# Two-layer transformer block on one core: one exp and one maximum for a pair of heads, and PSUM banks from a plan

## The chip, the cores and the metric

The kernel runs on one core of a Trainium2 chip. The metric is the device time of one execution in microseconds. Its engines are TensorE (PE; PEld is its weight load), VectorE (DVE), ScalarE (ACT), GpSimd (POOL), and SyncE (SP), which issues most transfers. TensorE writes its results into PSUM, which has eight banks of 512 fp32 values per partition.

## The reference

The input is x, 4 x 1024 x 128 in fp32. Two layers follow each other, and both add two branches to x that read the same normalized xn:

```python
xn = _layernorm(x)
x = x + _L0_attn_ref(xn, ...) + _L0_ffn_ref(xn, ...)
xn = _layernorm(x)
x = x + _L1_attn_ref(xn, ...) + _L1_ffn_ref(xn, ...)
```

Layer 0's attention has 16 heads of 8 dimensions, rotary Q and K, scores / sqrt(8), a softmax over 1024 keys, weights times V, and an output projection with bias. Its feed-forward is a mixture of 8 experts (128 to 512 to 128, Relu), of which each token uses the best two, weighted by a softmax. Layer 1's attention has the same heads, no rotation, and is causal. Its feed-forward is gated (silu(gate) * up, 352 wide), with inputs and weights rounded to FP4 in blocks of 16 with a scale per block.

## The kernel before, in words

A class `Plan` writes out the order of all work by hand rules before anything is emitted. The work of each batch and layer is a phase; there are eight, in the order `PHASES` (layer, batch): (0,0), (0,1), (1,0), (0,2), (1,1), (0,3), (1,2), (1,3). The kernel is a list of 491 slots, and every engine goes through the slots in order.

A slot can hold a *step* and a *quad*, and 436 of them hold both; 12 slots ahead of the first step hold a quad at most, and 12 at the end no quad.

- A step (`scores`, L930) is the scores of four heads (a group g) for one tile of 128 keys and 512 queries: four matmuls of kind E, keys on the partitions, each into a bank of its own. `exps` (L790) on ScalarE turns each into weights in `PR`. The step's product with V (PV, eight matmuls into the bank `pO`, which is no part of the round) comes one slot later and waits for all four exps. In layer 1 the tiles on the diagonal are narrower (512, 384, 256, 128 columns), and two small matmuls per pair add the mask.
- A quad is the same four heads with queries on the partitions, and serves the row maxima, 12 slots ahead of the steps that need them: four matmuls of kind M (`maxima` on TensorE, L955), and four reductions (`maxima` on VectorE, L1137) into `mparts`. In layer 1 the quads on the diagonal add the mask in the same operation (L1153) and write to `junk`. The finished maxima (`combine`, `mtr`) are put under the queries in `QX` by small transfers, so that the scores come out with the maximum subtracted.
- Everything else that passes through PSUM is an item of `xs`: projections (`pj`), the values (`v`), the experts' first and second product (`unit`, `y`), gate and up (`gu`), transposes (`xT`, `mtr`, `fin`, `of`, `turn`), and so on. Over both kinds of engine that empty them, 93 of the 436 slots have none, 173 one, 152 two and 18 three. `unit` is emptied by four Relu operations on ScalarE, `y` by one copy.

TensorE's order in a slot: E of heads 0 and 1, M of heads 0 and 1, PV of the step before, E of heads 2 and 3, M of heads 2 and 3, then the slot's `xs`. ScalarE's: exps 0 and 1, what the slot has besides, exps 2 and 3, evacuations. VectorE's: maxima 0 and 1, small steps, maxima 2 and 3, `combine`, small steps, evacuations.

Seven banks (`RING = 7`, tiles `ring0` to `ring6`) serve E, M and `xs`. `number` lists all fills in TensorE's order in `plan.ring`, and the bank of an item is its place in that list modulo 7. `vacant` (L918) makes TensorE wait until the item seven places earlier has been emptied: for an exp (`s_ex`), a maximum (`s_mr`) or an evacuation (`s_freed`). For a pair both waits stand ahead of both matmuls.

Of the kernel before, what the change touches and what calls it, by code (L numbers as in the profile page):

```python
# [34 lines left out]
class Plan:  # L35
# [214 lines left out]
    def number(self):  # L250
        self.steps, self.quads, self.outs, self.mtrs, self.combines, self.masks = {}, {}, {}, {}, {}, {}
        self.xs, self.by, self.fins, self.ring = {}, {}, {}, []
        self.parts, self.parts0, self.pools = {}, {}, {}
        self.at = {"E": {}, "M": {}, "X": {}}
        taken = {"A": 0, "D": 0}
        mid = 0
        for s in self.slots:
# [11 lines left out]
            for pair in range(2):  # L269
                for kind, key, n in (("E", s["step"], self.steps), ("M", s["quad"], self.quads)):  # L270
                    if key is not None:
                        for j in (2 * pair, 2 * pair + 1):
                            k = 4 * n[key] + j
                            self.at[kind][k] = len(self.ring)
                            self.ring.append((kind, k))
            for e in s["xs"]:
# [4 lines left out]
                taken[who] += 1  # L281
                self.at["X"][k] = len(self.ring)
                self.ring.append(("X", e))
# [9 lines left out]
            for e in s["pool"]:  # L293
                if e[0] == "round" and e[-1] == POOL_STEPS - 2:
                    self.pools[e[1:-1]] = len(self.pools)

    def bank(self, kind, k):
        return self.at[kind][k] % RING

# [4 lines left out]
def two_layer_block(nc, x, wqa0, wqb0, wka0, wkb0, wv0, wo0, gate_w, gate_b, w1, b1, w2, b2wo,  # L304
# [27 lines left out]
    with ctx:  # L332
# [3 lines left out]
        def ps(name, width):  # L336
            return ctx.enter_context(nc.psum_tensor(name, [P, width], f32))
# [91 lines left out]

        ring = [ps(f"ring{i}", HALF) for i in range(RING)]  # L430
        pO = ps("pO", HALF)
# [86 lines left out]
        def wide(t, n):  # L518
            return t[:, 0:n // BLK].rearrange("p (n o) -> p n o", o=1).to_broadcast([P, n // BLK, BLK])

        def bank(e):
            return ring[plan.bank("X", plan.xs[e])]

# [25 lines left out]
        with nc.Block() as block:  # L549
# [235 lines left out]
            def _(act):  # L785
# [4 lines left out]
                def exps(s, js):  # L790
# [12 lines left out]
                    if n >= 2:  # L803
                        act.wait_ge(s_pv, n - 1)
                    for j in js:
                        k = 4 * n + j
                        act.wait_ge(s_e, k + 1)
                        nc.scalar.activation(PR[:, n % 2, HALF * j + off:HALF * j + HALF],  # L808
                                             ring[plan.bank("E", k)][:, off:HALF], ACT.Exp,
                                             scale=SCALE).then_inc(s_ex, 1)  # L810

# [103 lines left out]
            def _(pe):  # L915
                pe.wait_ge(s_wA, 16 * len(loads_a))

                def vacant(kind, k):  # L918

                    r = plan.at[kind][k] - RING  # L920
                    if r >= 0:
                        was, of = plan.ring[r]
                        if was == "E":
# [46 lines left out]
                for s in plan.slots:  # L970
# [24 lines left out]
                    for e in s["xs"]:  # L995
                        vacant("X", plan.xs[e])
                        dst = bank(e)
# [120 lines left out]
            def _(dve):  # L1118
# [18 lines left out]
                def maxima(s, js):  # L1137
                    if s["quad"] is None:
                        return
                    p, g, qt, kh = s["quad"]  # L1140
                    layer = PHASES[p][0]
                    for j in js:
                        k = 4 * plan.quads[s["quad"]] + j
# [3 lines left out]
                        dve.wait_ge(s_m, k + 1)  # L1147
                        if layer == 0 or P * (qt + 1) > HALF * (kh + 1):
                            v.tensor_reduce(dst, src[:, 0:w], axis=X, op=ALU.max).then_inc(s_mr, 1)  # L1149
                        else:  # L1150
                            if k >= 2:
                                dve.wait_ge(s_mr, k - 1)
                            v.tensor_tensor_reduce(out=junk[k % 2][:, 0:w], in0=src[:, 0:w],  # L1153
                                                   in1=diag[:, HALF - w:HALF], scale=1.0, scalar=NEG,
                                                   op0=ALU.add, op1=ALU.max, accum_out=dst).then_inc(s_mr, 1)

# [350 lines left out]
```

## Time and profile before

| | |
|---|---|
| time, median of 3 runs | 1646.52 us (1646.3 to 1650.8) |
| the profiled execution's own time, and its span | 1650.6 us, 1648.9 us |
| PE busy | 1477.5 us (90%) |
| PEld busy | 623.0 us (38%) |
| DVE busy | 1342.0 us (81%), 3450 instructions |
| ACT busy | 1131.9 us (69%), 2612 instructions |
| POOL busy | 579.7 us (35%) |
| mean granted TensorE clock | 0.944 of full speed |

Busy times are the union of an engine's instructions, as shares of the span. A PE that is busy isn't PE at its peak, since the ends of its matmuls are modelled. In the listing by line a helper's line (L504, L507, L510) stands for all that call it; the tiles tell them apart: `ring<-QX,KX 50*128` is an E matmul, `ring<-KX,QX 48*128` an M matmul, `pO<-PR,VX` is PV, L808 the exps, L1149 and L1153 the maxima.

### The profile page before, as it was taken

To read this page: it belongs to the slowest core of one execution; us is meant where nothing else is said; L and a number is where in the kernel's file an instruction comes from. 1 tells how busy PE (TensorE), PEld (TensorE's weight loads), DVE (VectorE), ACT (ScalarE), POOL (GpSimd) and SP (SyncE) were. 2 spreads that over 40 slices of the span, in tenths; PEclk is the share of its full clock that TensorE was granted. 3 is DMA by queue.
4 is the path that set the end of the run, shared out by engine and by line. 5 is a ranking of instruction groups with operands and counts; after the bars stand their busy time and mean duration, and the time that the engine had idled before them with its cause. 6 is when DMAs were issued, how large, how long until landed. Compare 5 with 4: busy or idle time off the path is not lost.

```text
span 1648.9 us, 34553 instructions
## 1 busy us (share of the span) xinstructions
PE 1477.5 (90%) x10685; PEld 623.0 (38%) x10685; DVE 1342.0 (81%) x3450; ACT 1131.9 (69%) x2612; POOL 579.7 (35%) x532
## 2 busy tenths in 40 slices
PE   3688989997999999998999999989999989889996
PEld 1121334442434554433343444334444433334432
DVE  7999877786887778898888878879887878887990
ACT  2167678786788556777878756767887845766675
POOL 4003302003063353733434361221624473644520
PEclk8599999998999989999999999999999987999998
DMA  8202264323263135231711225223462100500000
GB/s 246 56 7 60 78 164 116 89 80 89 55 180 96 35 113 127 69 89 49 185 39 44 63 61 152 66 82 103 147 137 65 39 24 1 154 2 15 2 2 14
DMA packets 162915, 131.80 MB, mean 80 GB/s; under 512 B 30825, under 2 KB 130098, under 8 KB 162738
## 3 DMA queue, kind: packets, MB, share of 16 engines
q1 hardware_dynamic: 158642, 121.19, 27.2%
q0 software_dynamic: 4096, 8.40, 1.7%
q8 instruction: 93, 1.52, 0.4%
q14 instruction: 84, 0.69, 0.1%
HBM read 88.50 MB, written 40.50 MB: 78 GB/s over the span
## 4 chain that ended last, share of the span: by engine, by line
PE 64%; DVE 18%; ACT 6%; issue 5%; POOL 4%; DMA 1%; SPq 1%; another core or an unknown queue 0%; DVEq 0%; ACTq 0%; POOLq 0%
PE ring L504 41%; PE pO L504 19%; DVE mparts L1149 10%; PE ring L507 4%; ACT PR L808 4%; DVE junk L1153 1%; ACT hid L875 1%; DVE xn L1216 1%; DVE xr L1329 1%; DVE hs L1441 1%; DVE stats L1199 1%; DVE hs L1440 1%; POOL rstd L700 1%; POOL ra L707 0%; POOL parts L715 0%
## 5 line engine op out<-in xcount | busy, mean ns | idle before, releaser
L808 ACT ACTIVATE PR<-ring 128x512 f32<-128x512 f32 (+3 forms) x1792 | 875.9, 557 | 279.8 <-PE ring L504 267.1
L1149 DVE TENSOR_REDUCE mparts<-ring 128x1 f32<-128x512 f32 x1280 | 806.8, 682 | 122.1 <-PE ring L504 108.6
L504 PE MATMUL pO<-PR,VX 128*18 128x512 f32 (+3 forms) x3584 | 444.7, 569 | 9.2 <-ACT PR L808 8.5
L504 PE MATMUL ring<-KX,QX 48*128 48x512 bf16 (+3 forms) x1792 | 339.4, 373 | 82.3 <-ACT PR L808 32.4
L504 PE MATMUL ring<-QX,KX 50*128 50x512 bf16 (+3 forms) x1792 | 335.7, 371 | 36.7 <-DVE mparts L1149 20.3
L504 PEld LDWEIGHTS ring<-QX,KX 50*128 50x128 bf16 x1792 | 89.6, 93 | 481.7 <-DVE mparts L1149 175.2
L1153 DVE CUSTOM_DVE_ANT_0 junk<-ring,diag 128x384 bf16<-128x384 f32 (+3 forms) x512 | 227.8, 486 | 53.6 <-PE ring L504 46.3
L504 PEld LDWEIGHTS ring<-KX,QX 48*128 48x128 bf16 x1792 | 96.5, 94 | 181.5 <-DVE mparts L1149 54.1
L758 POOL TENSOR_SCALAR bq<-bq 128x352 f32<-128x352 f32 (+1 forms) x40 | 47.1, 1177 | 333.9 <-ACT bq L912 322.7
L731 POOL DMA_INDIRECT rows_in<-xn,at x64 | 62.6, 978 | 257.2 <-PE pO L504 166.0
L875 ACT ACTIVATE hid<-ring,b1r 128x128 f32<-128x128 f32 x368 | 104.9, 369 | 36.8 <-PE ring L504 36.2
L747 POOL DMA_INDIRECT ra<-rows_out,at x64 | 61.0, 953 | 170.8 <-PE pO L504 125.5
L504 PEld LDWEIGHTS pO<-PR,VX 128*18 128x18 f32 x3584 | 60.7, 97 | 142.3 <-issue 108.0
L504 PE MATMUL ring<-yx,w1r 128*128 128x128 f32 x736 | 108.0, 291 | 6.9 <-DMA b1r<-in_b 6.3
L504 PEld LDWEIGHTS ring<-yx,w1r 128*128 128x128 f32 x736 | 92.6, 197 | 31.6 <-issue 19.0
L504 PE MATMUL ring<-w2r,hid 128*128 128x128 f32 x736 | 99.2, 279 | 0.0
L504 PEld LDWEIGHTS ring<-w2r,hid 128*128 128x128 f32 x736 | 95.3, 200 | 0.9 <-ACT PR L808 0.9
L510 ACT ACTIVATE yx<-ring 128x256 f32<-128x256 f32 (+1 forms) x96 | 36.2, 377 | 58.1 <-PE ring L504 48.3
L504 PE MATMUL ring<-identb,laterb 128*128 128x128 bf16 x512 | 74.8, 229 | 0.0
L767 POOL TENSOR_TENSOR bq<-hq,bq 128x352 f32<-128x352 f32 x64 | 59.8, 934 | 4.8
L772 POOL TENSOR_SCALAR yq<-yq 128x352 f32<-128x352 f32 (+1 forms) x40 | 60.3, 1506 | 3.3
L715 POOL TENSOR_TENSOR parts<-rb,parts 128x512 bf16<-128x512 f32 x30 | 34.7, 1155 | 74.0 <-ACT parts L510 74.0
(164 smaller groups left out, 1406.1 us busy)
## 6 DMA issues: line engine op xcount, KB each, us to landing
scratch<-parts SPq DMA_DIRECT2D x96, 256.0 KB, 3.7
w1r<-in_w SPq DMA_DIRECT2D x92, 256.0 KB
w2r<-in_w SPq DMA_DIRECT2D x92, 256.0 KB
QX<-scratch SPq DMA_DIRECT2D x128, 96.0 KB, 3.2
KX<-scratch SPq DMA_DIRECT2D x64, 192.0 KB, 4.0
xg<-rows_in SPq DMA_DIRECT2D x92, 64.0 KB
rows_out<-yx SPq DMA_DIRECT2D x92, 64.0 KB
QX<-mT SPq DMA_DIRECT2D x256, 2.0 KB
```

Of the source, the lines that this page charges most:

```text
L504: return nc.tensor.matmul(dst, lhsT, rhs, start=start, stop=stop, **kw)
L507: return nc.tensor.transpose(dst, src, ident[0:src.shape[0], 0:src.shape[0]])
L510: return nc.scalar.activation(dst, src, ACT.Copy)
L731: nc.gpsimd.indirect_dma_start(xs[b % 2], bass.IndirectOffsetOnAxis(at[b % 2][:, c:c + 1], 0), xn[0][:, c % T, :], None).then_inc(s_sc[b], 16)
L747: nc.gpsimd.indirect_dma_start(yg[:, D * t:D * t + D], None, ys[b % 2], bass.IndirectOffsetOnAxis(at[b % 2][:, c:c + 1], 0)).then_inc(s_yg ...
L758: ins = nc.gpsimd.tensor_scalar(b_, b_, 1.0, None, ALU.max)
L767: ins = nc.gpsimd.tensor_tensor(b_, dst, b_, ALU.subtract)
L772: ins = nc.gpsimd.tensor_scalar(y, y, SHIFT, SHIFT, ALU.add, ALU.subtract)
L808: nc.scalar.activation(PR[:, n % 2, HALF * j + off:HALF * j + HALF], ring[plan.bank("E", k)][:, off:HALF], ACT.Exp, scale=SCALE).then_inc( ...
L875: ins = nc.scalar.activation(hid[N % 2][:, P * fc:P * fc + P], src[:, P * fc:P * fc + P], ACT.Relu, bias=b1r[N % 2][:, fc:fc + 1])
L1149: v.tensor_reduce(dst, src[:, 0:w], axis=X, op=ALU.max).then_inc(s_mr, 1)
L1153: v.tensor_tensor_reduce(out=junk[k % 2][:, 0:w], in0=src[:, 0:w], in1=diag[:, HALF - w:HALF], scale=1.0, scalar=NEG, op0=ALU.add, op1=ALU ...
```

## The change: one operation for two heads, and a placed pair of banks

- The seven banks become one tile `ring` of 7 x 512 columns; `both` gives a view [128, 2, n] over the banks of items k and k+1.
- `exps` issues one activation over two banks where it issued two, waits for both score matmuls, and counts `s_ex` up by two when it ends.
- `maxima` on VectorE issues one reduction over [128, 2, 512] into two columns of `mparts`, except for layer 1's quads on the diagonal, which stay as they were. 320 of the 448 quads are not on the diagonal. `s_mr` goes up by two. The places of the maxima within `mparts` are the same as before.
- `place_banks` replaces the fixed round. A unit is a pair (two neighbouring banks) or an item of `xs` (one bank). For each unit in TensorE's order `choose` tries the four places that were given out longest ago, looks ahead over the next five units in all, and takes the place with the least sum of max(0, 4 - ago) squared, where ago is the number of units since a bank of the place was last given out. `was` keeps, for each item, what its bank held before, and `vacant` waits for that.

Orders of work, matmuls, transfers and their placement in slots are not changed.

```diff
--- before.py
+++ after.py
@@ -251,7 +251,7 @@
         self.steps, self.quads, self.outs, self.mtrs, self.combines, self.masks = {}, {}, {}, {}, {}, {}
         self.xs, self.by, self.fins, self.ring = {}, {}, {}, []
         self.parts, self.parts0, self.pools = {}, {}, {}
-        self.at = {"E": {}, "M": {}, "X": {}}
+        self.banks = {}
         taken = {"A": 0, "D": 0}
         mid = 0
         for s in self.slots:
@@ -271,7 +271,6 @@
                     if key is not None:
                         for j in (2 * pair, 2 * pair + 1):
                             k = 4 * n[key] + j
-                            self.at[kind][k] = len(self.ring)
                             self.ring.append((kind, k))
             for e in s["xs"]:
                 who = "D" if e[0] in ("pj", "lg", "rt", "mtr", "fin", "gu", "down", "fp") else "A"
@@ -279,7 +278,6 @@
                 self.xs[e] = k
                 self.by[e] = (who, taken[who])
                 taken[who] += 1
-                self.at["X"][k] = len(self.ring)
                 self.ring.append(("X", e))
                 if e[0] == "fin":
                     self.fins[e[1:]] = len(self.fins)
@@ -293,9 +291,40 @@
             for e in s["pool"]:
                 if e[0] == "round" and e[-1] == POOL_STEPS - 2:
                     self.pools[e[1:-1]] = len(self.pools)
+        self.place_banks()
 
     def bank(self, kind, k):
-        return self.at[kind][k] % RING
+        return self.banks[kind, k]
+
+    def choose(self, used, units, now):
+
+
+        if not units:
+            return 0, None
+        width = units[0]
+        places = sorted(range(RING - width + 1), key=lambda b: max(used[b:b + width]))[:4]
+        best = None
+        for b in places:
+            ago = now - max(used[b:b + width])
+            then = used[:b] + [now] * width + used[b + width:]
+            cost = max(0, 4 - ago) ** 2 + self.choose(then, units[1:], now + 1)[0]
+            if best is None or cost < best[0]:
+                best = cost, b
+        return best
+
+    def place_banks(self):
+
+        units = [self.ring[i:i + (1 if self.ring[i][0] == "X" else 2)] for i in range(len(self.ring))
+                 if self.ring[i][0] == "X" or self.ring[i][1] % 2 == 0]
+        used, holds = list(range(-RING, 0)), {}
+        self.banks, self.was = {}, {}
+        for now, unit in enumerate(units):
+            b = self.choose(used, [len(u) for u in units[now:now + 5]], now)[1]
+            for i, item in enumerate(unit):
+                self.banks[item] = b + i
+                self.was[item] = holds.get(b + i)
+                holds[b + i] = item
+                used[b + i] = now
 
 
 PLAN = Plan()
@@ -427,7 +456,8 @@
         xqT = sb("xqT", [P, S])
         hqT = sb("hqT", [P, FC1, P])
 
-        ring = [ps(f"ring{i}", HALF) for i in range(RING)]
+        ring_all = ps("ring", RING * HALF)
+        ring = [ring_all[:, HALF * i:HALF * i + HALF] for i in range(RING)]
         pO = ps("pO", HALF)
 
         s_x0 = [sem(f"s_x{i}") for i in range(B)]
@@ -518,8 +548,13 @@
         def wide(t, n):
             return t[:, 0:n // BLK].rearrange("p (n o) -> p n o", o=1).to_broadcast([P, n // BLK, BLK])
 
+        def both(kind, k, lo, hi):
+
+            a, b = plan.bank(kind, k), plan.bank(kind, k + 1)
+            return ring_all[:, :].rearrange("p (b n) -> p b n", n=HALF)[:, a:b + 1, lo:hi]
+
         def bank(e):
-            return ring[plan.bank("X", plan.xs[e])]
+            return ring[plan.bank("X", e)]
 
         def filled(e):
             return plan.xs[e] + 1
@@ -802,12 +837,11 @@
                         act.wait_ge(s_x, filled(("wT", 2)))
                     if n >= 2:
                         act.wait_ge(s_pv, n - 1)
-                    for j in js:
-                        k = 4 * n + j
-                        act.wait_ge(s_e, k + 1)
-                        nc.scalar.activation(PR[:, n % 2, HALF * j + off:HALF * j + HALF],
-                                             ring[plan.bank("E", k)][:, off:HALF], ACT.Exp,
-                                             scale=SCALE).then_inc(s_ex, 1)
+                    k = 4 * n + js[0]
+                    act.wait_ge(s_e, k + 2)
+                    dst = PR[:, n % 2, HALF * js[0]:HALF * js[0] + 2 * HALF].rearrange("p (j n) -> p j n", n=HALF)
+                    nc.scalar.activation(dst[:, :, off:HALF], both("E", k, off, HALF), ACT.Exp,
+                                         scale=SCALE).then_inc(s_ex, 2)
 
                 for s in plan.slots:
                     exps(s, (0, 1))
@@ -917,9 +951,8 @@
 
                 def vacant(kind, k):
 
-                    r = plan.at[kind][k] - RING
-                    if r >= 0:
-                        was, of = plan.ring[r]
+                    if plan.was[kind, k]:
+                        was, of = plan.was[kind, k]
                         if was == "E":
                             pe.wait_ge(s_ex, of + 1)
                         if was == "M":
@@ -993,7 +1026,7 @@
                     scores(s, 1)
                     maxima(s, 1)
                     for e in s["xs"]:
-                        vacant("X", plan.xs[e])
+                        vacant("X", e)
                         dst = bank(e)
                         if e[0] == "xT":
                             _, p, h = e
@@ -1139,20 +1172,23 @@
                         return
                     p, g, qt, kh = s["quad"]
                     layer = PHASES[p][0]
+                    if layer == 0 or P * (qt + 1) > HALF * (kh + 1):
+                        k, i = 4 * plan.quads[s["quad"]] + js[0], TH * (js[0] // 2) + qt % TH
+                        dve.wait_ge(s_m, k + 2)
+                        v.tensor_reduce(mparts[layer][:, qt // TH, i:i + 2 * TH + 1:2 * TH, kh], both("M", k, 0, HALF),
+                                        axis=X, op=ALU.max).then_inc(s_mr, 2)
+                        return
                     for j in js:
                         k = 4 * plan.quads[s["quad"]] + j
                         w = HALF if layer == 0 else min(HALF, P * (qt + 1) - HALF * kh)
                         dst = mparts[layer][:, qt // TH, TH * (2 * (j % 2) + j // 2) + qt % TH, kh:kh + 1]
                         src = ring[plan.bank("M", k)]
                         dve.wait_ge(s_m, k + 1)
-                        if layer == 0 or P * (qt + 1) > HALF * (kh + 1):
-                            v.tensor_reduce(dst, src[:, 0:w], axis=X, op=ALU.max).then_inc(s_mr, 1)
-                        else:
-                            if k >= 2:
-                                dve.wait_ge(s_mr, k - 1)
-                            v.tensor_tensor_reduce(out=junk[k % 2][:, 0:w], in0=src[:, 0:w],
-                                                   in1=diag[:, HALF - w:HALF], scale=1.0, scalar=NEG,
-                                                   op0=ALU.add, op1=ALU.max, accum_out=dst).then_inc(s_mr, 1)
+                        if k >= 2:
+                            dve.wait_ge(s_mr, k - 1)
+                        v.tensor_tensor_reduce(out=junk[k % 2][:, 0:w], in0=src[:, 0:w],
+                                               in1=diag[:, HALF - w:HALF], scale=1.0, scalar=NEG,
+                                               op0=ALU.add, op1=ALU.max, accum_out=dst).then_inc(s_mr, 1)
 
                 def weight_step(k):
 
```

## Rows read from the trace of the kernel before

**Rows 1.** The page: span, busy us (share) and instructions, shares of the chain.
```profile
span 1648.9 us, 34553 instructions
...
PE 1477.5 (90%) x10685; PEld 623.0 (38%) x10685; DVE 1342.0 (81%) x3450; ACT 1131.9 (69%) x2612; POOL 579.7 (35%) x532
...
PE 64%; DVE 18%; ACT 6%; issue 5%; POOL 4%; DMA 1%; SPq 1%; another core or an unknown queue 0%; DVEq 0%; ACTq 0%; POOLq 0%
PE ring L504 41%; PE pO L504 19%; DVE mparts L1149 10%; PE ring L507 4%; ACT PR L808 4%; DVE junk L1153 1%; ACT hid L875 1%; DVE xn L1216 1%; DVE xr L1329 1%; DVE hs L1441 1%; DVE stats L1199 1%; DVE hs L1440 1%; POOL rstd L700 1%; POOL ra L707 0%; POOL parts L715 0%
```

**Rows 2.** Waits of PE: waiting line, releaser: us in total, times, longest.
```profile
PE ring L504 <- DVE mparts L1149: 39.9, 69, 2.7
PE ring L504 <- ACT PR L808: 38.8, 85, 2.0
```

**Rows 3.** Timeline from 118 us: start, length, engine, operation, tiles, count [idle before].
```profile
120.90 0.39 PE L504 MATMUL ring<-QX,KX 50*128 50x512 bf16 x2
...
121.39 2.06 ACT L808 ACTIVATE PR<-ring 128x512 f32<-128x512 f32 x4 [0.54 <-PE ring L504]
...
121.46 0.39 PE L504 MATMUL ring<-QX,KX 50*128 50x512 bf16 x2
...
122.13 0.39 PE L504 MATMUL ring<-KX,QX 48*128 48x512 bf16 x2 [0.28 <-ACT PR L808]
...
122.53 1.05 PE L504 MATMUL pO<-PR,VX 128*18 128x512 f32 x8
...
123.51 0.39 PE L504 MATMUL ring<-QX,KX 50*128 50x512 bf16 x2
```

**Rows 4.** The chain from 118 to 136 us: shares by line, start, length, what.
```profile
by line: DVE mparts L1149 44.6%; PE pO L504 23.2%; PE ring L504 19.3%; ACT PR L808 6.7%; issue 2.7%; DVE otok L1431 2.7%; DVE mT L1420 1.5%; DVE linv L1424 1.5%; DVE mT L1419 1.1%; ACTq L807 0.0%
...
121.39 0.60 ACT PR L808
121.99 0.14 issue
```

**Rows 5.** Groups by line and shape: busy us, mean ns, idle before.
```profile
L1149 DVE TENSOR_REDUCE mparts<-ring 128x1 f32<-128x512 f32 x1280 | 806.8, 682 | 122.1 <-PE ring L504 108.6 <-issue 8.0 <-DVE xr L1449 0.6
L808 ACT ACTIVATE PR<-ring 128x512 f32<-128x512 f32 x1408 | 752.5, 604 | 191.2 <-PE ring L504 184.2 <-PE pO L504 2.7 <-issue 1.2
...
L1153 DVE CUSTOM_DVE_ANT_0 junk<-ring,diag 128x512 bf16<-128x512 f32 x128 | 82.2, 686 | 7.3 <-PE ring L504 5.6 <-DVE xr L1449 1.0
...
L808 ACT ACTIVATE PR<-ring 128x128 f32<-128x128 f32 x128 | 28.4, 277 | 23.5 <-PE ring L504 23.3
...
L1153 DVE CUSTOM_DVE_ANT_0 junk<-ring,diag 128x128 bf16<-128x128 f32 x128 | 31.6, 286 | 15.6 <-PE ring L504 14.1 <-issue 0.7
```

**Rows 6.** Timeline of DVE before the first scores.
```profile
28.70 1.31 DVE L1161 TENSOR_REDUCE am<-PR 128x70 f32<-128x1120 f32 x1
...
45.39 15.03 DVE L1149 TENSOR_REDUCE mparts<-ring 128x1 f32<-128x512 f32 x25
```

**Rows 7.** Timeline of three slots: M23 and the fill behind it.
```profile
180.62 0.38 PE L504 MATMUL ring<-KX,QX 48*128 48x512 bf16 x2
...
180.94 0.44 PE L507 MATMUL ring<-ident,otok 128*128 128x128 f32 x2
...
667.07 2.13 ACT L808 ACTIVATE PR<-ring 128x512 f32<-128x512 f32 x4
...
667.88 0.34 PE L504 MATMUL ring<-KX,QX 48*128 48x384 bf16 x2
...
668.27 0.66 PE L507 MATMUL ring<-ident,oT 128*128 128x128 f32 x4
...
1598.40 0.39 PE L504 MATMUL ring<-QX,KX 50*128 50x512 bf16 x2
```

**Rows 8.** Exps of the first slot (timeline) and the last (chain).
```profile
79.30 2.07 ACT L808 ACTIVATE PR<-ring 128x512 f32<-128x512 f32 x4 [1.83 <-PE ring L504]
...
1604.33 0.61 ACT PR L808
```

## The prediction

> **What bounds the kernel now.** First the page's busy times and its chain: TensorE is busy 90% of 1648.9 us, VectorE 81%, ScalarE 69%, and the chain that ended last runs 64% through PE, 18% through DVE and only 6% through ACT [rows 1]. So PE's in-order stream sets the time, and the reader should see that the two engines whose operations become fewer are mostly not the ones that end last. Second, what PE waits for: it stood idle 39.9 us for maxima and 38.8 us for exps, each wait short [rows 2]. These are waits for a bank to come free, and both edits change them: how long one operation holds a bank, and which operation is waited for. Third, the timeline of a few slots, to see how such a wait is built.
>
> Names used below, in PE's order inside a slot: E01 (scores of heads 0, 1), M01 (products for their maxima), PV of the step before, E23, M23, then the slot's 0 to 3 other fills, X. A prime marks the next slot.
>
> **The wait in a slot without X.** Before, slot items take banks in a round of seven, so each waits for the item seven back. With no X the second bank of M01' was that of head 2 of E23, seven items earlier: M01' waits for the *first* exp of E23. The trace shows it: E23 starts at 120.90, its exp at 121.39 and ends at 121.99 after 0.60; 0.14 us later, at 122.13, M01' starts. Four exps take 2.06 us, so they follow each other at (2.06 - 0.60)/3 = 0.49, the second ends at 121.39 + 0.49 + 0.60 = 122.48, and PV starts at 122.53, 0.05 later; E23' follows at 123.51, 0.98 later [rows 3, 4]. The loop is 0.49 + 0.60 + 0.14 + 0.40 + 0.98 = 2.61 us, exactly the distance from 120.90 to 123.51.
>
> After, pairs lie in two neighbouring banks. Just before M01' the last three pairs (E23, M23, E01') hold six of seven banks, so whatever the plan chooses, M01' has to take at least one bank of a pair; the oldest is E23, and its banks come free only when the one exp over both ends. One term follows.
>
> **Cost of a merged operation.** The exps take 604 ns at 512 columns and 277 ns at 128, 0.85 ns a column [rows 5]; so one over 2 x 512 lasts 0.60 + 0.44 = 1.04 us against 1.09 for two in a row. I take 0.05 us saved a pair. Nothing in the trace is this form, so the bounds are 0 (a second bank costs what a second instruction does) and 0.17 (604 - 436 ns, the whole fixed part). For the maxima the slope comes from L1153, (686 - 286)/384 = 1.04 ns, 533 ns for 512, and one lasts 682 ns [rows 5]; 25 in a row take 15.03 us, (15.03 - 0.68)/24 = 0.60 each [rows 6], so the second of a pair saves 0.60 - 0.53 = 0.065 us. Bounds 0 and 0.15 (682 - 533). That many results cost no stop of their own is shown by the reduction into 70 outputs, 1120 columns in 1.31 us [rows 6]. All in all 896 exp pairs save 45 us of ACT and 640 maxima pairs 42 us of DVE: 87 us of engine time, most of it off the path. Both matmuls of a pair start together (one entry of 0.39 us for two [rows 3]), so waiting for the second before either starts costs nothing. The waits left out and the bank view itself cost nothing.
>
> The Trainium skill ("Perfetto Trace Analysis", Optimizing Scalar/DVE Operations) has a price for the same thing, about 125 ns for a VectorE operation that reads PSUM, where the rows give 65. By it term C below would be 17 us instead of 9, and the time 1657. The same section says that if these engines are not saturated but cause bubbles on others, breaking instructions up may let work finish sooner; that speaks against this change, and the 0.14 us behind the first exp of a pair is such a case.
>
> **Term A, slots without X.** After, the exp over E23 ends 0.05 earlier than its second did, M01' starts 0.14 behind it, and PV at least 0.32 behind M01' (the pitch from an M pair to the next fill, 180.62 to 180.94 [rows 7]); PV now starts 0.05 behind the second exp. Delay: -0.05 + 0.14 + 0.32 - 0.05 = 0.36 us, the loop goes from 2.61 to 2.97. There are 92 slots without X that a slot with maxima follows; I went through each and took the part of this delay that its own PV would feel: 77 of them, the first with the exp at 79.30, the last with the one at 1604.33 [rows 8], 23 us together (0.30 each; narrower exps of layer 1 lose less). E01' will also wait for both maxima of M01 instead of the first, but M01' behind it is later anyway.
>
> **Term B, M23'.** Before, its second bank is always that of E01' head 0, whatever number of X stood between (E1', M0', M1', E2', E3' and M2' stand between, so it is seven back). After, E01', M01' and E23' hold six banks, so M23' always waits for the whole exp of E01'. Where ACT is behind, in slots after a `unit` with its four Relus, this shows: the four exps begin at 667.07, M23' starts at 667.88 and the next fill at 668.27 [rows 7]. That next fill already waited for the second exp (667.07 + 0.51 + 0.60 = 668.18), so M23' itself may slip by 0.4 and the stream slips less: exp end 668.11, + 0.14 M23', + 0.32 the fill at 668.57, 0.3 late. Gone through slot by slot it is 34 us in 132 of the 436 slots that have both kinds; the fill behind M23' is at 180.94 in the first, at 1598.40 in the last [rows 7]; 75 of them, 25 us, follow a `unit`. ACT is what is late there, and it gets two exps a slot cheaper: 132 x 2 x 0.05 = 13 us back. B is 34 - 13 = 21 us.
>
> What is queued behind both waits on PE: PV and E23' behind M01', the X fills and E01'' behind M23'. So each delay reaches ACT and DVE again through the next fills. A + B = 44 us.
>
> **How much of it stays.** A slot that DVE alone holds up swallows it. DVE, POOL and the rest but PE, ACT and issue make up a quarter of the chain [rows 1], and around the slots shown it is more: DVE's maxima are 44.6% of the local chain [rows 4]. I let three quarters stay: +33 us.
>
> **Term C, DVE on the path.** Maxima are 10% of the chain [rows 1], 165 us, at 0.60 that is 275 of them, 137 pairs x 0.065 = -9 us (0 to -20 by the bounds). **Term D, ACT.** Its exps are 4%, 66 us, at 0.49 135 of them, 68 pairs x 0.05 = -3 us (0 to -11). **Start and end.** Twelve slots of maxima alone, 24 pairs x 0.065, and twelve at the end without maxima, 24 pairs x 0.05: -3 us. **The X fills.** With one X a slot they can keep the seventh bank and wait for nobody; but the X that followed a late M23 was gated by its own exp, and now by M23' before it, so I give no gain beyond B.
>
> Sum: +33 - 9 - 3 - 3 = +18 us. Against the profiled execution's own 1650.6 this is 1669 (its span of 1648.9 becomes 1667); that run stood 4 us above the median of 1646.5, so the forecast is 1646.5 + 18 = 1664.5, rounded 1665 us, 1.1% slower.
>
> **Rivals.**
> *Saved time decides, faster.* Its place is the stretches where DVE never idles, as around 118 to 130, and ACT behind a `unit`. For it: the local chain [rows 4] and DVE's 81%. If merged operations save their upper bounds there (C -20, D about -6) and only a quarter of A + B stays (+11), the sum with the ends (-3) is -18: 1629 us. It decides from the point where about a third of A + B (15 of 44) or less stays at my prices. Against it: the loop of 2.61 us is met to the hundredth by exps and PE alone [rows 3]. Chance 0.20.
> *No difference.* Between 23% and 45% of A + B stays (10 to 20 us against gains of 15), or both sides small: 1642 to 1651. Chance 0.14.
> *Placement breaks the banks up, still slower.* 170 slots have two or more X. Two X in different pairs' banks leave no two neighbouring free ones, and a pair waits for an X filled two units ago, whose evacuation may be four Relus behind. At 0.2 us a slot that adds 34 us: 1699 us. Against it: the plan looks five units ahead and punishes this. Chance 0.10.
> *My forecast*, slower by 5 to 45 us: 0.56.
>
> **From this to the numbers.** A difference under 0.3% (5 us) can't be told from none here. Slower is 0.56 + 0.10 = 0.66, same 0.14, faster 0.20. The likeliest case alone spans 1652 to 1690 (all or half of A + B, C from 0 to -20). The range must hold part of the faster case too: 1636 to 1690 leaves out some 0.10 below and 0.07 above.
>
> **What would show it.** Right: in slots without X, M01' starts 0.14 us behind an exp of 1.04 us and the distance between two PVs is near 2.97; M23' starts no earlier than the end of the exp of E01'; ACT's and DVE's busy time fall by about 45 and 42 us while the span grows; the chain's ACT share rises and its DVE share falls. Wrong: an exp over two banks at 1.09 us or more, or a merged maximum below 1.1; M01' starting before the exp's end (then the plan found a bank that I say isn't there); PE waits for exps below 38.8 us; a shorter span with DVE's chain share falling by more than its saved time.

## The result, and the profile after

The changed kernel takes 1702.88 us (median of 4 runs, 1694.35 to 1714.42) against 1646.41 us: ratio 1.035, 95% interval [1.027, 1.043]. Run once more beside later experiments it was 1696.8 against 1637.1 us: 1.037 [1.033, 1.040]. The forecast was 1665 us and the range ended at 1690. The direction is right, the size a third of what came.

The page's busy times and what TensorE waited for, which answer to [rows 1, 2]:

```profile
span 1693.2 us, 33587 instructions
...
PE 1473.2 (87%) x10685; PEld 632.7 (37%) x10685; DVE 1314.6 (78%) x2810; ACT 1086.1 (64%) x1716; POOL 579.9 (34%) x532
...
PE 28%; issue 8%; DVE 8%; ACT 7%; POOL 4%; DMA 0%; SPq 0%; ACTq 0%; another core or an unknown queue 0%; DVEq 0%; POOLq 0%
```
```profile
PE ring L534 <- ACT PR L843: 80.5, 159, 2.0
PE ring L534 <- DVE mparts L1178: 44.1, 85, 1.6
...
PE pO L534 <- ACT PR L843: 8.2, 13, 1.0
```

ACT lost 46 us of busy time (45 forecast) and DVE 27 (42 forecast); the span grew by 44 us. PE waits 80.5 us for exps where it waited 38.8, in 159 waits where there were 85, and 44.1 us for maxima of L1178 where there were 39.9 for L1149. The work got cheaper and the waiting dearer. The chain of this page (its last line above) is followed over only 55% of the span, so the forecast signs "ACT's share rises, DVE's falls" can be read only within that part: ACT has 7 of 55 and DVE 8 of 55, where they had 6 and 18 of 99.

The forms of the merged operations (mean ns behind the busy time), to be read against [rows 5]:

```profile
L1178 DVE TENSOR_REDUCE mparts<-ring 128x2 f32<-128x1024 f32 x640 | 773.9, 1222 | 182.9 <-PE ring L534 160.8 <-issue 14.0 <-DVE xr L1485 0.5
```
```profile
L843 ACT ACTIVATE PR<-ring 128x1024 f32<-128x1024 f32 x704 | 711.5, 1026 | 238.0 <-PE ring L534 224.4 <-PE pO L534 3.9 <-issue 2.9
...
L843 ACT ACTIVATE PR<-ring 128x256 f32<-128x256 f32 x64 | 24.4, 384 | 30.2 <-PE ring L534 27.8 <-PE pO L534 1.2
```

One exp over two banks lasts 1026 ns and one maximum 1222, about as priced (1040 and 1215). The maxima of this form were busy for 806.8 us before and for 773.9 now, 0.05 us less a pair where the forecast took 0.065.

The timeline of a slot without X, against [rows 3]:

```profile
120.42 0.39 PE L534 MATMUL ring<-QX,KX 50*128 50x512 bf16 x2
...
120.65 0.38 PE L534 MATMUL ring<-KX,QX 48*128 48x512 bf16 x2
...
120.96 1.02 ACT L843 ACTIVATE PR<-ring 128x1024 f32<-128x1024 f32 x1 [1.08 <-PE ring L534]
...
121.00 0.39 PE L534 MATMUL ring<-QX,KX 50*128 50x512 bf16 x2
121.17 1.23 DVE L1178 TENSOR_REDUCE mparts<-ring 128x2 f32<-128x1024 f32 x1 [0.31 <-PE ring L534]
```
```profile
122.13 0.39 PE L534 MATMUL ring<-KX,QX 48*128 48x512 bf16 x2 [0.74 <-ACT PR L843]
...
122.45 1.05 PE L534 MATMUL pO<-PR,VX 128*18 128x512 f32 x8
...
123.44 0.39 PE L534 MATMUL ring<-QX,KX 50*128 50x512 bf16 x2
```

E23 starts at 120.42, the one exp over it at 120.96 and, after 1.02 us, it ends at 121.99; M01' starts at 122.13, 0.14 behind it, PV at 122.45, E23' at 123.44. The loop is 3.02 us where the forecast had 2.97 and the kernel before 2.61. The surplus of 0.05 lies in the start of the exp, 0.54 behind its matmuls instead of 0.49.

And term B, in the same step as the second slot of [rows 7]:

```profile
682.30 1.96 ACT L843 ACTIVATE PR<-ring 128x1024 f32<-128x1024 f32 x2
...
682.65 0.39 PE L534 MATMUL ring<-QX,KX 50*128 50x512 bf16 x2
...
683.49 0.34 PE L534 MATMUL ring<-KX,QX 48*128 48x384 bf16 x2 [0.45 <-ACT PR L843]
...
683.76 0.66 PE L537 MATMUL ring<-ident,oT 128*128 128x128 f32 x4
```

The two exps begin at 682.30, M23' at 683.49 with a wait of 0.45 us for the exp, and the fill behind it at 683.76. E23' had gone at 682.65, and without the wait M23' would have followed 0.26 us behind it, as it did before (667.62 to 667.88). Counted from the first exp, the fill behind M23' stands at 1.46 us where it stood at 1.20 (667.07 to 668.27): 0.26 late, 0.3 forecast.

One thing about sizes: within one kernel the time follows the mean granted clock of the execution. The changed kernel's four runs were 1695.0 and 1694.4 us at a clock of 0.956 and 0.957, and 1714.4 and 1710.8 at 0.937 and 0.939. The profiled execution of before stood at 0.944 and that of after at 0.956, so the two spans (44 us apart) show less than the medians (56). What follows is told by ratios to runs of before that were interleaved with them on the same chip, times 1640 us for microseconds; not all kernels ran on the same chip, so a difference between two ratios is less sure than either.

### The profile page after: what moved, and what is told of

Its sections match the earlier page's. It is cut to its first block, busy times and chain, and to the rows that moved or that the text cites. A ratio compares the mean times of both kernels' runs of the same rounds, so it can differ in the third digit from the quotient of the medians.

```text
span 1693.2 us, 33587 instructions
## 1 busy us (share of the span) xinstructions
PE 1473.2 (87%) x10685; PEld 632.7 (37%) x10685; DVE 1314.6 (78%) x2810; ACT 1086.1 (64%) x1716; POOL 579.9 (34%) x532
## 3 DMA queue, kind: packets, MB, share of 16 engines
q1 hardware_dynamic: 158642, 121.19, 26.5%
## 4 chain that ended last, share of the span: by engine, by line
PE 28%; issue 8%; DVE 8%; ACT 7%; POOL 4%; DMA 0%; SPq 0%; ACTq 0%; another core or an unknown queue 0%; DVEq 0%; POOLq 0%
PE ring L534 18%; PE pO L534 8%; ACT PR L843 5%; DVE mparts L1178 4%; PE ring L537 2%; ACT hid L909 1%; DVE junk L1189 1%; POOL bq L802 1%; POOL yq L807 0%; POOL yq L804 0%; DVE xn L1252 0%; POOL ra L782 0%; DVE hs L1477 0%; POOL hq L799 0%; POOL bq L793 0%
## 5 line engine op out<-in xcount | busy, mean ns | idle before, releaser
L843 ACT ACTIVATE PR<-ring 128x1024 f32<-128x1024 f32 (+3 forms) x896 | 824.3, 934 | 345.8 <-PE ring L534 327.9
L1178 DVE TENSOR_REDUCE mparts<-ring 128x2 f32<-128x1024 f32 x640 | 773.9, 1222 | 182.9 <-PE ring L534 160.8
L534 PEld LDWEIGHTS ring<-KX,QX 48*128 48x128 bf16 x1792 | 101.9, 94 | 233.5 <-ACT PR L843 103.3
L807 POOL TENSOR_SCALAR yq<-yq 128x352 f32<-128x352 f32 (+1 forms) x40 | 60.2, 1506 | 3.3
L804 POOL TENSOR_SCALAR yq<-yq 128x352 f32<-128x352 f32 (+1 forms) x40 | 60.1, 1502 | 0.1
```

The source lines that it names most:

```text
L534: return nc.tensor.matmul(dst, lhsT, rhs, start=start, stop=stop, **kw)
L804: ins = nc.gpsimd.tensor_scalar(y, y, -1.0, 1.0, ALU.max, ALU.min)
L807: ins = nc.gpsimd.tensor_scalar(y, y, SHIFT, SHIFT, ALU.add, ALU.subtract)
L843: nc.scalar.activation(dst[:, :, off:HALF], both("E", k, off, HALF), ACT.Exp, scale=SCALE).then_inc(s_ex, 2)
L1178: v.tensor_reduce(mparts[layer][:, qt // TH, i:i + 2 * TH + 1:2 * TH, kh], both("M", k, 0, HALF), axis=X, op=ALU.max).then_inc(s_mr, 2)
```

## Experiments

All kernels but the first three of the table keep the fixed round of seven banks; "merged" means one operation over two banks, where the pair doesn't wrap from bank 6 to bank 0. That leaves 765 of the 896 exp pairs and 546 of the 640 maxima pairs, so about one pair in seven stays two operations. They are made from the changed kernel by a test in front of each merged operation and, for the fixed round, two lines in `place_banks`:

```diff
+        self.banks = {item: n % RING for n, item in enumerate(self.ring)}
+        self.was = {item: self.ring[n - RING] if n >= RING else None for n, item in enumerate(self.ring)}
+        return
```

| kernel | merged | ratio to before | us |
|---|---|---|---|
| changed kernel, again | all, plan's banks | 1.037 [1.033, 1.040] | +60 |
| place_exp | exps, plan's banks | 1.035 [1.032, 1.039] | +58 |
| place_only | none, plan's banks | 1.029 [1.025, 1.032] | +47 |
| round_whole | none, waits for whole pairs | 1.041 [1.039, 1.044] | +68 |
| round_both | exps and maxima | 1.030 [1.026, 1.033] | +49 |
| round_exp | exps | 1.026 [1.022, 1.029] | +42 |
| exp_ab | exps over E01, and E23 without X | 1.022 [1.016, 1.028] | +36 |
| exp23_nox | exps over E23 without X (term A) | 1.010 [1.006, 1.013] | +16 |
| exp01 | exps over E01 (term B) | 1.007 [1.005, 1.010] | +12 |
| exp23_x2 | exps over E23, two or more X | 0.999 [0.997, 1.001] | -1 |
| round_max | maxima | 1.006 [1.003, 1.009] | +10 |
| max23_x2 | maxima over M23, two or more X | 1.007 [1.005, 1.010] | +12 |
| max_not2x | the other maxima | 1.005 [1.002, 1.008] | +8 |
| max01_nox | maxima over M01 without X | 1.000 [0.998, 1.002] | 0 |
| max_wait_two | none, first maximum waits for both | 0.999 [0.997, 1.002] | -1 |
| together | where one later pair takes both banks | 0.999 [0.997, 1.000] | -2 |
| best_try | the same, and E23 wherever there is an X | 1.000 [0.998, 1.002] | 0 |

### Which part of the change costs: placement, exps, maxima

`place_only` gives out banks by the plan and leaves every operation single (part of its diff against the changed kernel):

```diff
+        MERGED = {"E": lambda k: False, "M": lambda k: False}
...
+                    if not merged("E", 4 * n + js[0]):
+                        for j in js:
+                            k = 4 * n + j
+                            act.wait_ge(s_e, k + 1)
+                            nc.scalar.activation(PR[:, n % 2, HALF * j + off:HALF * j + HALF],
+                                                 ring[plan.bank("E", k)][:, off:HALF], ACT.Exp,
+                                                 scale=SCALE).then_inc(s_ex, 1)
+                        return
```

(and the maxima likewise). 

> Banks from the plan as in the changed kernel, but every exp and every maximum is an operation of its own, as before. Theory 1 (what costs is that a pair's banks come free together, so M01' and M23' wait for the second exp of a pair instead of the first): the banks still come as a pair, so the waits stay and nothing is saved: 40 to 60 us slower than before, as slow as the changed kernel or up to 10 us slower. Theory 2 (the longer single operation costs, the placement is innocent): within 10 us of before. In the trace: by theory 1 M01' in a slot without X starts 0.14 us behind the second exp of E23.

It is 2.9% slower, with not one operation merged. Its trace has the sign that theory 1 asked for: in 73 of the 92 slots without X, M01' starts 0.13 to 0.16 us behind the end of the *second* exp of E23, where in the trace of before it starts so behind the end of the *first* in 66 of 92. The other three take the fixed round and merge one kind or both.

> The fixed round of seven banks as before; the two exps of a pair are one operation wherever the pair doesn't wrap from bank 6 to bank 0 (about 6 of 7 pairs); maxima as before. Theory 1: the merged exp frees both banks at its end, so M01' and M23' wait as in the changed kernel in 6 of 7 cases: 25 to 45 us slower than before. Theory 2 agrees in sign. A rival, that it is the plan's distances that cost (pairs taking banks given out too recently, in slots with two X above all): under 10 us slower than before.

> The fixed round as before, exps as before; the two maxima of a pair are one operation wherever the pair doesn't wrap (about 6 of 7 of the 640 pairs). Theory 1: only E01' waited for a first maximum, and M01' behind it waits for an exp anyway, so the saved 0.065 us a pair shows where DVE is on the path: 2 to 10 us faster than before. Rival (a merged maximum frees its banks later, and this costs as the exps do): 5 to 15 us slower.

> The fixed round as before, both kinds merged wherever the pair doesn't wrap. Against the changed kernel only the placement differs (and 1 pair in 7 stays two operations). Theory 1: 20 to 40 us slower than before, that is 5 to 20 us faster than the changed kernel. If the plan's placement has a cost of its own beyond the pairing: 25 us or more faster than the changed kernel.

Merged exps alone cost 2.6% with the old banks, the placement alone 2.9% with the old operations, and all of it 3.5 to 3.7%. The two don't add up. The likely reason is that they do the same thing by two ways: either of them makes TensorE wait until both halves of a pair are done, which the next run tries by itself. Merged maxima cost 0.6% where 2 to 10 us of gain were expected: theory 1 missed there. `round_both`, at +49 [43, 54], lies above its 20 to 40 us; the 8 to 11 us that separate it from the changed kernel are within the 5 to 20 of theory 1. About as much would come of the unmerged seventh alone: 49 us taken from six sevenths of the pairs to all are 57 (an estimate).

### The waits by themselves

`round_whole` changes no operation, bank or order, only what `vacant` waits for:

```diff
-                            pe.wait_ge(s_ex, of + 1)
+                            pe.wait_ge(s_ex, (of | 1) + 1)
-                            pe.wait_ge(s_mr, of + 1)
+                            pe.wait_ge(s_mr, (of | 1) + 1)
```

> The fixed round and all operations single, as before; only TensorE's waits differ: where it waited for one item of an older pair it now waits for both. No operation, bank or order differs. If the whole loss is in waiting for the second half: 40 to 50 us slower than before. If the merged operations or the placement add what the waits don't explain: 25 to 35 us.

It is 4.1% slower, more than the changed kernel. Its busy times, its waits and a slot without X:

```profile
span 1717.3 us, 34553 instructions
...
PE 1487.5 (87%) x10685; PEld 640.4 (37%) x10685; DVE 1353.5 (79%) x3450; ACT 1137.8 (66%) x2612; POOL 579.9 (34%) x532
```
```profile
PE ring L537 <- ACT PR L852: 83.6, 161, 2.4
PE ring L537 <- DVE mparts L1205: 51.1, 90, 2.8
```
```profile
119.47 0.39 PE L537 MATMUL ring<-QX,KX 50*128 50x512 bf16 x2
...
119.95 1.08 ACT L852 ACTIVATE PR<-ring 128x512 f32<-128x512 f32 x2 [0.46 <-PE ring L537]
...
120.84 0.39 PE L537 MATMUL ring<-QX,KX 50*128 50x512 bf16 x2 [0.76 <-DVE mparts L1205]
...
121.19 0.39 PE L537 MATMUL ring<-KX,QX 48*128 48x512 bf16 x2
...
121.51 1.05 PE L537 MATMUL pO<-PR,VX 128*18 128x512 f32 x8
...
122.49 0.39 PE L537 MATMUL ring<-QX,KX 50*128 50x512 bf16 x2
```

DVE and ACT are as busy as before the change, PE waits 83.6 us for exps. E23 starts at 119.47, two single exps begin at 119.95, M01' starts at 121.19 behind the second of them, and E23' at 122.49: a loop of 3.02 us, that of the changed kernel. E01', between them, had waited for the maxima of M01 and left at 120.84; in this slot both waits end almost together. So waiting for the second half is enough for the whole loss. It even costs more than the changed kernel. With the fixed round 709 pairs take their banks from two different older pairs and now wait for both in whole, where the plan's list has 118 such; that this is the 1.3% between `round_whole` and `place_only` was not tried, and in the plan's list 387 fills still wait only for the first half of the pair that they wait for last.

### Terms A and B one at a time, and together

The test in front of the merged exp is `k % 4 == 2` in slots without X for A, and `k % 4 == 0` for B.

> The fixed round; the only merged operation is the exp over E23 in slots without X (88 pairs that don't wrap, some 75 of them with an M01' that waits). This is term A by itself. If a delayed M01' stays in the stream in full: 88 x 0.3 = 22 to 28 us slower than before. If a quarter or more of it is swallowed, as I let it be in the prediction: 12 to 20 us slower.

> The fixed round; the only merged operation is the exp over E01 (388 pairs that don't wrap). This is term B by itself: M23' waits for the whole exp, the fill behind it slips less, ACT saves 388 x 0.05 us. Expected 12 to 20 us slower than before. If M23' is harmless because the next fill waited for the second exp anyway: under 5 us.

A alone costs 16 us [10, 22], B alone 12 [7, 16], with 88 of the 92 and 388 of the 448 pairs merged. Both intervals hold what the forecast had after its discount of a quarter (17 and 16). The discount shows in the trace of A alone: measured from one E23 to the next, the 92 slots without X take 21.7 us longer than before, nearly the 23 us of term A before the discount, and the whole kernel only 16, so other slots win some back (the two traces stand at clocks of 0.952 and 0.944, so this split is rough). The timeline of A alone:

```profile
121.52 0.39 PE L537 MATMUL ring<-QX,KX 50*128 50x512 bf16 x2
...
122.06 1.02 ACT L861 ACTIVATE PR<-ring 128x1024 f32<-128x1024 f32 x1 [1.01 <-PE ring L537]
122.98 1.08 ACT L854 ACTIVATE PR<-ring 128x512 f32<-128x512 f32 x2
...
123.23 0.39 PE L537 MATMUL ring<-KX,QX 48*128 48x512 bf16 x2 [0.88 <-ACT PR L861]
...
123.55 1.05 PE L537 MATMUL pO<-PR,VX 128*18 128x512 f32 x8
123.64 1.29 DVE L1207 TENSOR_REDUCE mparts<-ring 128x1 f32<-128x512 f32 x2 [0.19 <-PE ring L537]
```

E23 at 121.52, the exp over it 122.06 to 123.08, M01' at 123.23 and PV at 123.55: the loop of 3.0 us, made by this one merged operation (the exps over E01 behind it, L854, are still two).

> The fixed round; exps merged for all E01 and for E23 in slots without X (terms A and B in one kernel, maxima as before). If the two add up: 28 to 34 us slower than before. If they help each other (the whole run with merged exps was 42 us slower, the two alone 15 and 15): 36 to 44 us. What is then left to the run with all exps merged is E23 in slots with X.

Together they cost 36 us [26, 45] (by the median 45), against 28 for the sum of the two. TensorE's waits for exps in it, L861 the merged and L854 the single ones:

```profile
PE ring L537 <- ACT PR L861: 74.6, 126, 2.4
...
PE ring L537 <- ACT PR L854: 14.2, 42, 0.7
```

The interval holds the sum as well as 40 us. That A and B help each other is likely by the medians and not shown: the runs compared are three of 1682 to 1684 us at a clock of 0.942 to 0.945 and two of 1660 and 1663 at 0.962.

### Where merged maxima cost

> The fixed round, exps as before; maxima merged as in the run with maxima alone, but not those of M23 in slots with two or more X (447 merged pairs instead of about 550). If what made merged maxima slower is that M01' after two X waits for the second maximum of M23: 3 to 10 us faster than that run, which is no slower than before. If the merged maximum costs in another place: as slow as that run, 5 to 15 us slower than before.

Its interval holds part of both answers: 0.2 to 0.8% slower than before, against 0.3 to 0.9% for all maxima. So three runs with one wait each followed.

> The fixed round; the only merged operation is the maximum over M23 in slots with two or more X (99 pairs), where M01' waits for the first maximum of M23. If the prediction's term C has its sign wrong because of this wait: 5 to 10 us slower than before. If the loss of merged maxima lies elsewhere: within 3 us.

> The fixed round; the only merged operation is the maximum over M01 in slots without X (64 pairs), where E01' waits for the first maximum of M01. The prediction called this wait harmless, because M01' behind E01' waits for an exp: within 3 us of before. If it is the other part of what merged maxima cost: 3 to 8 us slower.

> The fixed round, exps and maxima all single operations as before; the first maximum of a pair waits for both matmuls of the pair. It isolates the later start. If both products are there together, as I priced it: no change, and the first maximum still starts 0.41 us behind its matmul. If the second product comes 0.1 us later: the start moves to 0.51 us, and the time rises by 3 to 12 us.

The wait of M01' for the first maximum of M23, in slots with two or more X, carries it: 99 merged operations, 0.7% slower. One such slot, PE and DVE of `max23_x2`:

```profile
651.83 0.39 PE L537 MATMUL ring<-KX,QX 48*128 48x512 bf16 x2
...
652.53 0.51 DVE L1420 TENSOR_REDUCE am<-hs 128x22 f32<-128x352 f32 x1
...
653.16 1.22 DVE L1197 TENSOR_REDUCE mparts<-ring 128x2 f32<-128x1024 f32 x1
...
653.25 0.34 PE L537 MATMUL ring<-QX,KX 50*128 50x384 bf16 x2
...
654.52 0.23 PE L537 MATMUL ring<-KX,QX 48*128 48x128 bf16 x2 [0.72 <-DVE mparts L1197]
```

M23 starts at 651.83. Before, DVE would empty its two banks one by one, and M01' needs only the first. Here the maximum starts at 653.16 behind a small step and lasts 1.22; E01' went at 653.25, and M01' stands until 654.52. Over the 170 slots with two or more X the distance from E01' to M01' grew by more than 0.1 us in 43, by 0.54 us at most and 15.8 us in all, against the profile of before. E01' waiting for both maxima of M01 costs nothing, as forecast (`max01_nox`): in its trace the 92 E01' behind a slot without X start 17.8 us later in all, counted from M23, and the distance from them to M01' shrinks by 14.0. In `max_wait_two` the first maximum starts 0.45 us behind its matmuls on an idle DVE (median of 239), where it was 0.41 and 0.51 had been feared, and the time doesn't move.

The prediction hadn't seen it, although the same plan of the round gives it: with two X the seventh fill before the second of M01' is the first of M23 (all 43 slots have exactly two; with three X both banks of M23 go to M01').

The trace of `max_not2x` also shows where its own 0.5% goes at least in part. Without X the first bank of M23 goes to E23', so E23' now waits for the whole maximum over M23. In 13 of the 92 slots without X the distance from PV to E23' grew by more than 0.1 us, 5.4 us in all, and in 11 of them E23' starts 0.15 us behind the end of a maximum; in `max01_nox`, where these maxima stay single, it grew in 2. No run has this wait alone.

### What is left: E23 with X, and maxima under the plan

> The fixed round; the only merged operation is the exp over E23 in slots with two or more X (143 pairs), where E01' waits for the first exp of E23. If this wait, for which the prediction has no term, is the rest of the run with all exps merged: 4 to 10 us slower than before. If the rest comes from A and B helping each other: within 3 us.

No difference: this wait has slack.

> Banks from the plan, exps merged, maxima as two operations. Under the plan a pair's two banks are waited for together in any case, so merging the maxima can only act through the operation itself. If the saved 0.065 us a pair counts (my term C): 5 to 9 us slower than the changed kernel. If the later start counts (a merged maximum starts 0.51 us behind its matmuls on an idle DVE, a single one 0.41): 3 to 12 us faster than the changed kernel.

> The changed kernel once more, on the chip of the following runs, so that they can be compared with it: 50 to 60 us slower than before.

Under the plan merging the maxima changes nothing (1.035 against 1.037, within either interval), so neither of the two expected answers came: under the plan most pairs are waited for in whole anyway, and neither the saved 0.065 us nor the later start shows. Merging the exps under the plan does add something: `place_exp` stands at 1.035 [1.032, 1.039] and `place_only` at 1.029 [1.025, 1.032], on two chips. The fills of the plan that still waited for a first half may be it; that was not tried.

### Merging only where nobody waits for a first half

```diff
+        def heirs(kind, k):
+            after = [plan.ring[spot[kind, j] + RING] for j in (k, k + 1) if spot[kind, j] + RING < len(plan.ring)]
+            return [(a, b // 2 if a != "X" else b) for a, b in after]
+        def together(kind, k):
+            h = heirs(kind, k)
+            return len(h) == 2 and h[0] == h[1]
```

> The fixed round; a pair is merged only if both of its banks go to the same later pair (or to the two halves of one), so that nobody waits for its first half alone: 162 exps and 250 maxima. Theory (all of the loss is in waits for a second half, the operations themselves are cheaper): no slower than before and up to 10 us faster. If a merged operation costs by itself: 3 us or more slower than before.

> The fixed round; exps over E23 merged in slots with at least one X (289 pairs), maxima merged only where both banks go to the same later pair (250 pairs): every place in which the runs showed no loss. If the saved engine time reaches the end anywhere: 2 to 8 us faster than before. If it is all hidden behind TensorE: within 3 us.

With 162 exps and 250 maxima merged the time is that of before (0.999, 1.000). The loss is gone, and no gain is seen: DVE and ACT are busy for 13 and 9 us less in `together` (1328.6 and 1123.2 us). How much of this reaches the end is not settled. By the forecast's own shares (21% of the maxima and 8% of the exps on the path) it would be 4 us, an estimate, and the interval of `together`, from 5 us faster to none, holds that; that of `best_try`, from 3 faster to 3 slower, hardly. No version beat the kernel before clear of noise.

## Why the prediction was wrong

*What bounds the kernel* held: TensorE's stream sets the time, and what it waits for decides. *The counting of banks* held: three pairs hold six banks, M01' without X starts 0.14 behind an exp of 1.03 us, the loop is 3.02 us; M23' waits for the whole exp of E01'. *The prices of the merged operations* held to 14 ns. That waiting for the second matmul costs nothing did not quite hold: an operation over the pair starts 0.05 us (exp) and 0.1 us (maximum) later; `max_wait_two`, where a first maximum starts 0.04 later, shows no time for it.

*Terms A and B, and how much of them stays*: forecast +33 us together, measured 36 [26, 45] with both (`exp_ab`), 16 and 12 alone. Right as far as it can be measured, in part by luck: "three quarters stay" was a guess, and 36 of 44 us or 28 of 44 fit it about equally.

*Term C is the step that failed.* "Maxima are 10% of the chain ... -9 us" counted merged maxima by their saved time alone, and the only wait for a first maximum that the text weighed was that of E01'. Measured: +10 us with the fixed round, carried by M01' waiting for M23 after two X (`max23_x2`, +12). In the changed kernel itself merging the maxima moves nothing (1.037 with it, 1.035 without, `place_exp`), where -9 us were forecast. Where no wait was added (`together`, `best_try`) no saving is seen either, though some 4 us can't be ruled out. With *terms D* and *start and end*, -6 us, it is the same: the forecast took 15 us off for savings, and no run shows any of them. A share of the chain isn't a price at which that engine's time can be sold; that TensorE had its next wait there is the likely reason and was not shown.

*The plan's placement had no term.* The forecast's slower rival feared pairs behind an X filled two units ago, at 1699 us. The number came, the mechanism didn't: in the list of banks that the plan gives out no unit takes a bank given out less than three units before. What the plan does in the 170 slots with two or more X is that M01' takes both banks of M23 in 112 and one in 48, and E01' both banks of E23 in 113 and one in 47. That its waits for whole pairs cost without any merging is shown by `place_only`. Against the fixed round with both kinds merged the changed kernel is some 0.6% slower by its two ratios (1.035 and 1.037 against 1.030), 8 to 11 us; whether this comes from these slots or from the pairs that `round_both` leaves unmerged was not tried.

Added up: 36 (A, B) + 6 (round_exp over exp_ab) + 7 (maxima on top) + 8 to 11 (plan, or the last seventh of the pairs) = 57 to 60 us, against +18 forecast: 15 us of savings that weren't seen, 3 us more of A and B, and 21 to 24 us that had no term. That these are waits for whole pairs too is what `round_whole` and `max23_x2` speak for; only their sum is clear of noise, since each is a difference of two ratios about as large as its uncertainty.

The Trainium skill ("Perfetto Trace Analysis", Optimizing Scalar/DVE Operations) says that if these engines aren't saturated but cause bubbles on others, breaking instructions up may let work finish sooner. The trace agrees: `round_exp` turns 765 pairs of exps into one operation each and costs 42 us, with ACT busy 65%. The price of about 125 ns for a VectorE operation on PSUM, which the Trainium skill gives in the same section, would have made the forecast worse (1657 us, the prediction's estimate).

Open stays what makes up the rest of the 0.5% of `max_not2x` beyond the 5 us at E23' (the first X behind a merged M01 in slots with two X is a wait of the same kind that no run has alone); whether A and B help each other; what merging the exps adds under the plan; and whether the last 0.6% of the changed kernel is the plan's.

## What to carry to other kernels

Before merging two operations that empty two buffers, list for each buffer who takes it next; if one of the two goes to somebody alone, the merged operation makes that one wait for the second half, and the 0.4 us a slot of that (a loop of 3.02 us for 2.61) weighs more than 0.05 us saved. Giving two buffers out together does the same without any merging. Count such waits for every distance that the order produces, not only for the loop that is seen in the timeline, and give saved time on an engine that is mostly off the path no value until a run shows it.

## What the hardware showed that I hadn't expected

- An operation over a pair of banks starts later behind its matmuls than one over the first bank: ACT 0.54 instead of 0.49 us, DVE 0.52 (120.65 to 121.17 above) instead of 0.41 (123.23 to 123.64 in A's timeline). With single maxima that only wait for both matmuls it is 0.45. From an idle engine a merged maximum (0.52 + 1.22) thus ends 0.04 us after two single ones (0.41 + 1.29), and a merged exp (0.54 + 1.02) about with them (0.49 + 1.08); by these sums there is a saving only when the operation queues behind another.
- A maximum over two rows of 512 lasts 1222 ns and an exp 1026: the second bank adds 540 and 422 ns to the 682 and 604 of one bank, where 512 columns cost 533 and 436 by the slopes of [rows 5], so there is no stop between banks.
- The same kernel on the same chip moves by 22 us with its mean granted clock: `max_not2x` took 1634.8 us at 0.956 and 1657.0 at 0.938. A change of half a per cent needs many runs, or runs at one clock.
